# Blockwise FP4 quantiser: one Newton step fewer, and the square on VectorE instead of ScalarE

## The chip, the cores and the metric

One Trainium2 chip, 8 cores. Every core runs the same program on its own two sequences of the batch (4,096 tokens of 16 x 2,048). The metric is the device time of the slowest core in microseconds.

## What is computed

A transformer block on x (16 x 2048 x 1024, fp32): layer norm, then a linear-attention branch with an MLP (s) and an FP4-quantised gated FFN (g), joined as x + s * silu(g).

```python
def fp4_quant_dequant(x):            # blocks of 16 along the last axis
    scale = max(max(|xb|) / 6, 1e-12)
    xn = xb / scale
    idx = searchsorted([0.25, 0.75, 1.25, 1.75, 2.5, 3.5, 5.0], |xn|)
    return GRID[idx] * sign(xn) * scale     # GRID = 0, .5, 1, 1.5, 2, 3, 4, 6
def fp4_linear(x, w):
    return quant(x) @ quant(w).T

xn = layernorm(x)
# branch 1: rmsnorm, qkv, phi(t) = exp(-t*t/2), linear attention, projection,
#           then rmsnorm, conv1 (1024 -> 2048), gelu, conv2 (2048 -> 1024)
s = attn_block(xn)
# branch 2: inner size 2816
h = silu(fp4_linear(xn, w_gate)) * fp4_linear(xn, w_up)
g = silu(fp4_linear(h, w_down))
out = x + s * g
```

## The kernel before

The kernel writes its instructions into one list for each engine (`S.add("v", ...)` for VectorE, `"sc"` for ScalarE, `"pe"` for TensorE, `"sy"` for the DMA queue of SP). Each engine works through its list strictly in that order and waits on counting semaphores. So where an instruction stands in the list decides what it can hold up. A core has 32 tiles of 128 tokens. The stages run one after the other:

- P0: statistics of the layer norm. P1: qkv, attention and projection.
- P2, the convolution stage: 8 superblocks of 4 tiles. A superblock has a front (for each tile: load x2b, ScalarE casts it to x2f at L875, VectorE scales it at L878, 8 transposes and 8 copies), then 128 conv1 matmuls with 16 Gelus on ScalarE (L910, L919), then for each tile 32 conv2 matmuls (L938) and six VectorE instructions, the first of which is the bias add at L947. Between them the quantisation of the gate and up weights is pumped in: `pump(55)` behind each tile of the front and `pump(25)` behind each tile of the back takes that many steps of a generator. It works on 44 chunks of 128 rows x 1024 columns, each as one pair of quantisers of 512 columns. The chunks have a load and a store of their own on SP's queue.
- P25, the down-weight stage: 8 chunks of 128 x 2816, each as two pairs of 704 columns, with nothing else beside them.
- A1, the gate stage: for each tile VectorE normalises (L1031) and one pair of quantisers (512 columns) runs; then 8 transposes and 8 copies xqf on ScalarE (L1048, L1055), 48 gate matmuls (L1066) and 6 SiLUs on ScalarE (L1075).
- A2, the up stage: for each tile two loads (xqu at L1103, the gate at L1107), 48 up matmuls (L1120), 6 copies on ScalarE (L1129), the product gld * up on VectorE (L1132), two pairs of quantisers (704 columns) one behind the other; then, for the tile before, 22 transposes and 22 copies hqf (L1152, L1158) and the store of hqT_h (L1161). In the lists this "back" of tile t - 1 stands behind the "front" of tile t, and the loads of tile t + 1 stand behind the store of tile t - 1 on SP's queue.
- B: the down matmuls and the output.

The quantiser (`quant_gen`) is one chain. VectorE: maximum of each block (L648), scale (L651), a first guess for its reciprocal by integer arithmetic (L654 to L662), then Newton rounds of three small instructions each (L669, L672, L676), on one number a block (32 or 44 of them in a partition). Then u = x / scale (L682). ScalarE: u2 = u * u (L686, Square), Sign of u (L689), Sign of u2 against three thresholds (L692, L695, L698). VectorE compares u2 with four other thresholds (L701, L704, L707, L710: called "checks" below), adds the Signs (L713, L716), puts the two together (L719), multiplies the sign by the scale (L723) and writes the result (L728). `run_gens` and the chunk generator let two quantisers take turns, instruction by instruction.

A chunk of the pumped quantiser has 33 generator steps: number 1 to 5 for the maximum to the guess, 12 for the Newton rounds, 18 for u, 19 to 23 for the five ScalarE instructions, 24 to 27 for the checks, 28 to 32 for the rest and 33 for the store.

Of the kernel before, what the change touches and what calls it, by code (L numbers as in the profile page):

```python
# [11 lines left out]
AF = mybir.ActivationFunctionType  # L12
# [48 lines left out]
S = Sched()  # L61
# [60 lines left out]
def build():  # L122
    global S
    S = Sched()
# [21 lines left out]
    with ExitStack() as es:  # L146
# [28 lines left out]
        for nm, src, dst, csem in [("qkv", "L0_attn_qkv_w", "qkv_bf", "CQ"),  # L175
# [4 lines left out]
                  inc=csem, ev="cast_" + nm)  # L180
# [8 lines left out]
              waits=["iota_id"], inc="V", ev="identb")  # L189
# [4 lines left out]
        for oc in range(HID // P):  # L194
# [3 lines left out]
                inc="VR", ev=("ld_vrows" if oc == HID // P - 1 else None))  # L198
        S.add("v", lambda v: v.memset(ones1[:], 1.0), inc="V", ev="ones1")
        with ExitStack() as p0:  # L200
# [5 lines left out]
            for i, nm in enumerate(("s1", "s2", "gm", "pb", "c2b")):  # L206
                for h in range(2):
# [3 lines left out]
                        waits=["ones1", "ld_vrows"] + ([prev] if prev else []),  # L211
                        inc="PE", ev="repm%d_%d" % (i, h))
                    S.add("v", lambda v, nm=nm, h=h: v.tensor_copy(
                        reps[nm][:, 512 * h:512 * (h + 1)], rep_ps[:]),
                        waits=["repm%d_%d" % (i, h)], inc="V", ev="repc%d_%d" % (i, h))
                    prev = "repc%d_%d" % (i, h)
            for t in range(NT):
# [3 lines left out]
                    waits=[S.gev("p05v%d" % (t - 2), "V")], inc="XA%d" % b, ev="p05x%d" % t)  # L221
                S.add("sc", lambda sc, b=b: sc.activation(xsq[b][:], xa[b][:], AF.Square),
                      waits=["p05x%d" % t, S.gev("p05v%d" % (t - 2), "V")],
# [415 lines left out]
        def quant_gen(q, src_ap, dst_ap, W, waits_src, done_ev):  # L639
# [25 lines left out]
            yield  # L665
            yv = wi.bitcast(F32)
            prev = e("wi2")
            for it in range(4):
                S.add("v", lambda v, yv=yv, prev=prev: v.tensor_tensor(w2, sca, yv, op.mult),  # L669
                      waits=[prev], inc="V", ev=e("w2a%d" % it))  # L670
                yield
                S.add("v", lambda v, it=it: v.tensor_scalar(w2, w2, -1.0, 2.0, op.mult, op.add),  # L672
                      waits=[e("w2a%d" % it)], inc="V", ev=e("w2b%d" % it))
                yield
                dst = rec if it == 3 else w1
                S.add("v", lambda v, yv=yv, dst=dst, it=it: v.tensor_tensor(dst, yv, w2, op.mult),  # L676
                      waits=[e("w2b%d" % it)], inc="V", ev=e("nr%d" % it))
                yv = w1
                prev = e("nr%d" % it)
                yield  # L680
            rb = rec.rearrange("p nb -> p nb ()").broadcast_to([P, nb, 16])
            S.add("v", lambda v: v.tensor_tensor(  # L682
                u.rearrange("p (nb b) -> p nb b", b=16), x3, rb, op.mult),
                waits=[e("nr3")], inc="V", ev=e("u"))
            yield
            S.add("sc", lambda sc: sc.activation(u2, u, AF.Square),  # L686
                  waits=[e("u")], inc="SC", ev=e("u2"))
            yield
            S.add("sc", lambda sc: sc.activation(sgn, u, AF.Sign),  # L689
                  inc="SC", ev=e("sgn"))  # L690
            yield
            S.add("sc", lambda sc: sc.activation(s5, u2, AF.Sign, bias=thrB[:, 0:1]),  # L692
                  waits=[e("u2"), "thrB"], inc="SC", ev=e("s5"))
# [595 lines left out]
```

How the kernel before makes its waits and increments, by code:

```python
                def body(eng):  # L1261
                    for fn, waits, inc, amt in S.ops[key]:
                        for smn, val in waits:
                            eng.wait_ge(sems[smn], val)
                        ins = fn(eng)
                        if inc is not None and ins is not None:
                            ins.then_inc(sems[inc], amt)
```

## Time and profile before

| | us |
|---|---|
| median of the runs (2) | 7,250.89 |
| lowest, highest | 7,241.04, 7,260.75 |
| the profiled execution, its time | 7,273.16 |
| its span on the slowest core | 7,271.6 |
| spans of the eight cores | 7,212.9 to 7,271.6 |
| busy: VectorE | 3,821.7 (53%) |
| busy: TensorE matmul | 2,620.9 (36%) |
| busy: ScalarE | 2,226.5 (31%) |
| DMA, 16 engines, mean | 54 GB/s |

The profile shows one execution on its slowest core. Busy shares are means over stages that differ, so they say little by themselves; the windows by stage and the timeline say which wait ends last. A line such as L672 names the line of the kernel that issued an instruction. Timeline lines join neighbouring instructions of one kind ("x2"), and the bracket at their end tells how long the engine was idle before and what released it.

### The profile page before, as it was taken

To read this page: it belongs to the slowest core of one execution; us is meant where nothing else is said; L and a number is where in the kernel's file an instruction comes from. 1 tells how busy PE (TensorE), PEld (TensorE's weight loads), DVE (VectorE), ACT (ScalarE), POOL (GpSimd) and SP (SyncE) were. 2 spreads that over 40 slices of the span, in tenths; PEclk is the share of its full clock that TensorE was granted. 3 is DMA by queue.
4 is the path that set the end of the run, shared out by engine and by line. 5 is a ranking of instruction groups with operands and counts; after the bars stand their busy time and mean duration, and the time that the engine had idled before them with its cause. 6 is when DMAs were issued, how large, how long until landed. Compare 5 with 4: busy or idle time off the path is not lost.

```text
span 7271.6 us, 59859 instructions; the slowest of 8 cores (7212.9 to 7271.6 us)
## 1 busy us (share of the span) xinstructions
PE 2620.9 (36%) x10905; PEld 1125.2 (15%) x11098; DVE 3821.7 (53%) x9384; ACT 2226.5 (31%) x4379; POOL 3.2 (0%) x13
## 2 busy tenths in 40 slices
PE   0066456542303213373004445422222222222288
PEld 0022122211101101131001222111101110111033
DVE  0400320133576676525776666566676677667522
ACT  0133223321322322222224344323333333333211
POOL 0000000000000000000000000000000000000000
PEclk9988678866656656686556666655555555555599
DMA  8500010013011110010122222211101110111255
GB/s 98 139 24 24 33 46 21 18 44 77 28 39 34 37 38 31 33 32 26 48 56 80 79 85 82 88 50 41 41 27 41 41 41 27 41 41 41 70 168 174
DMA packets 227710, 396.17 MB, mean 54 GB/s; under 512 B 147861, under 2 KB 147989, under 8 KB 217626
## 3 DMA queue, kind: packets, MB, share of 16 engines
q1 hardware_dynamic: 226778, 375.57, 16.3%
q0 software_dynamic: 576, 16.78, 2.1%
q8 instruction: 111, 1.82, 0.1%
q14 instruction: 245, 2.01, 0.1%
HBM read 246.44 MB, written 145.33 MB: 54 GB/s over the span
## 4 chain that ended last, share of the span: by engine, by line
PE 29%; issue 25%; DVE 21%; ACT 11%; DMA 7%; SPq 5%; DVEq 1%; ACTq 0%
PE gps L1066 5%; PE ups L1120 5%; PE kvg_ps L394 4%; PE c1ps L910 3%; PE d_ps L1218 3%; SPq L195 2%; PE c2ps L938 2%; DMA xqu<-xqT_h 2%; PE q_ps L443 2%; PE prA L588 1%; ACT qb_s L695 1%; DVE gld L1132 1%; DMA hln<-hqT_h 1%; PE xp4t L1152 1%; DMA winw<-L_ffn_w_up 1%
## 5 line engine op out<-in xcount | busy, mean ns | idle before, releaser
L1152 PE MATMUL xp4t<-ident_b,hq 128*128 128x128 bf16 x704 | 178.8, 261 | 1368.1 <-ACT hqf L1158 1283.3
L1120 PE MATMUL ups<-wquT,xqu 128*128 128x512 bf16 (+1 forms) x1504 | 364.9, 410 | 243.3 <-DMA xqu<-xqT_h 208.3
L1132 DVE TENSOR_TENSOR gld<-gld,up 128x2816 f32<-128x2816 f32 x32 | 98.9, 3092 | 608.1 <-ACT up L1129 608.1
L363 DVE SCALAR_TENSOR_TENSOR xn<-xn,rstd_all,rep_s 128x1024 bf16<-128x1024 f32 x32 | 41.1, 1284 | 693.0 <-ACT xn L352 693.0
L890 PE MATMUL xp2t<-ident_b,xn 128*128 128x128 bf16 x256 | 65.1, 265 | 923.2 <-DVE xn L878 389.7
L1048 PE MATMUL xp3t<-ident_b,xq 128*128 128x128 bf16 x256 | 67.8, 265 | 893.9 <-DVE xq L728 864.8
L1066 PE MATMUL gps<-wqgT,xqf 128*128 128x512 bf16 (+1 forms) x1504 | 362.4, 408 | 31.7 <-ACT xqf L1055 31.7
L686 ACT ACTIVATE qb_u<-qb_u 128x704 f32<-128x704 f32 x128 | 101.1, 790 | 828.8 <-DVE qb_u L682 828.0
L1218 PE MATMUL d_ps<-wqdT,hln 128*128 128x512 bf16 x1379 | 322.2, 394 | 85.0 <-DMA hln<-hqT_h 80.7
L394 PE MATMUL kvg_ps<-qkvT,fmsup 128*128 128x512 bf16 x992 | 303.8, 471 | 29.7 <-ACT fmsup L378 25.0
L1152 PEld LDWEIGHTS xp4t<-ident_b,hq 128*128 128x128 bf16 x704 | 73.3, 104 | 1471.8 <-issue 1470.9
L910 PE MATMUL c1ps<-fm,conv1T 128*128 128x512 bf16 x1000 | 246.9, 410 | 102.7 <-ACT hddf L919 95.3
L938 PE MATMUL c2ps<-conv2T,hddf 128*128 128x512 bf16 x1004 | 228.6, 387 | 56.6 <-DVE s_t L964 18.1
L1129 ACT COPY up<-ups 128x512 f32<-128x512 f32 x192 | 105.4, 550 | 465.2 <-PE ups L1120 456.5
L686 ACT ACTIVATE qgw_u<-qgw_u 128x512 f32<-128x512 f32 x88 | 53.8, 629 | 604.4 <-DVE qgw_u L682 604.2
L1120 PEld LDWEIGHTS ups<-wquT,xqu 128*128 128x128 bf16 x1536 | 164.0, 108 | 441.3 <-issue 325.9
L1233 DVE TENSOR_TENSOR gfl<-gfl,sfl 128x1024 f32<-128x1024 f32 x32 | 39.2, 1226 | 335.1 <-ACT sfl L1230 335.1
L947 DVE TENSOR_TENSOR scc<-c2ps,rep_c2b 128x512 f32<-128x512 f32 x64 | 41.2, 686 | 326.0 <-PE c2ps L938 313.5
L1158 ACT COPY hqf<-xp4t 128x128 bf16<-128x128 bf16 x704 | 182.4, 265 | 86.5 <-PE xp4t L1152 53.8
L1066 PEld LDWEIGHTS gps<-wqgT,xqf 128*128 128x128 bf16 x1536 | 163.4, 108 | 227.9 <-issue 111.9
L1075 ACT ACTIVATE gate<-gps 128x512 f32<-128x512 f32 x192 | 107.8, 562 | 284.9 <-PE gps L1066 284.8
L596 DVE TENSOR_TENSOR x2w<-prA,rep_pb 128x512 f32<-128x512 f32 x32 | 22.1, 692 | 309.0 <-PE at L548 289.8
(243 smaller groups left out, 6874.9 us busy)
## 6 DMA issues: line engine op xcount, KB each, us to landing
xa<-x SPq DMA_DIRECT2D x160, 512.0 KB, 4.0
gate_h<-gate SPq DMA_DIRECT2D x32, 1408.0 KB, 5.7
gld<-gate_h SPq DMA_DIRECT2D x32, 1408.0 KB, 7.1
hqT_h<-hqf SPq DMA_DIRECT2D x32, 704.0 KB, 3.7
hln<-hqT_h SPq DMA_DIRECT2D x32, 704.0 KB, 5.7
out<-otl SPq DMA_DIRECT2D x32, 512.0 KB, 3.2
winw<-L_ffn_w_gate SPq DMA_DIRECT2D x22, 512.0 KB, 3.8
winw<-L_ffn_w_up SPq DMA_DIRECT2D x22, 512.0 KB, 3.9
```

What stands on the lines that cost most here:

```text
L195: S.add("sy", lambda sy, oc=oc: sy.dma_start(out=c1b_fm[:, oc:oc + 1], in_=g["L0_attn_conv1_b"][P * oc:P * (oc + 1)].rearrange("p -> p ()" ...
L394: S.add("pe", lambda pe, sup=sup, sp=sp, ic=ic, gg=gg: pe.matmul(kvg_ps[gg % 2][:], sup[:, 512 * ic + P * sp:512 * ic + P * (sp + 1)], qkv ...
L443: S.add("pe", lambda pe, sup=sup, qc=qc, ic=ic: pe.matmul(q_ps[0][:], qkvT[:, 3 * D * ic + P * qc:3 * D * ic + P * (qc + 1)], sup[:, 512 * ...
L686: S.add("sc", lambda sc: sc.activation(u2, u, AF.Square), waits=[e("u")], inc="SC", ev=e("u2"))
L910: S.add("pe", lambda pe, sup=sup, oc=oc, ic=ic: pe.matmul(c1_ps[oc % 2][:], conv1T[:, HID * ic + P * oc:HID * ic + P * (oc + 1)], sup[:, 5 ...
L938: S.add("pe", lambda pe, hdd=hdd, t=t, tt=tt, ic=ic, hh=hh: pe.matmul(c2_ps4[2 * (t % 2) + hh][:], hdd[:, 512 * ic + P * tt:512 * ic + P * ...
L1066: S.add("pe", lambda pe, b=b, ic=ic, cgo=cgo, cgw=cgw, cgi=cgi: pe.matmul(g_ps[cgi % 4][:, 0:cgw], xqf[b][:, P * ic:P * (ic + 1)], wqgT[:, ...
L1120: S.add("pe", lambda pe, b=b, ic=ic, cgo=cgo, cgw=cgw, cgi=cgi: pe.matmul(u_ps[cgi % 4][:, 0:cgw], xqu[b][:, P * ic:P * (ic + 1)], wquT[:, ...
L1132: S.add("v", lambda v, b=b: v.tensor_tensor(gld[b][:], gld[b][:], up_t[b][:], op.mult), waits=["a2_g%d" % t, "a2_ue%d_5" % t], inc="V", ev ...
L1152: S.add("pe", lambda pe, b=b, ic=ic: pe.transpose(xp4_ps[ic % 2], hq[b][:, P * ic:P * (ic + 1)], ident_b[:]), waits=tw, inc="PE", ev="a2_t ...
L1158: S.add("sc", lambda sc, b=b, ic=ic: sc.copy(hqf[b][:, P * ic:P * (ic + 1)], xp4_ps[ic % 2]), waits=fw, inc="SC", ev="a2_fme%d_%d" % (t, ic))
L1218: S.add("pe", lambda pe, b=b, t=t, ic=ic, hh=hh: pe.matmul(d_ps[2 * (t % 2) + hh][:], hln[b][:, P * ic:P * (ic + 1)], wqdT[:, D * ic + 512 ...
```

## The change

One Newton round of the quantiser is dropped (three instead of four). u * u is computed on VectorE by a product of u with itself instead of by Square on ScalarE. Sign of u on ScalarE, which stood behind Square and needed no wait of its own, now waits for u. Everything else, the numbers of steps taken by `pump` included, stays; a chunk of the pumped quantiser has 30 generator steps instead of 33.

```diff
             yv = wi.bitcast(F32)
             prev = e("wi2")
-            for it in range(4):
+            NRI = 3
+            for it in range(NRI):
                 S.add("v", lambda v, yv=yv, prev=prev: v.tensor_tensor(w2, sca, yv, op.mult),
...
-                dst = rec if it == 3 else w1
+                dst = rec if it == NRI - 1 else w1
...
             S.add("v", lambda v: v.tensor_tensor(
                 u.rearrange("p (nb b) -> p nb b", b=16), x3, rb, op.mult),
-                waits=[e("nr3")], inc="V", ev=e("u"))
-            yield
-            S.add("sc", lambda sc: sc.activation(u2, u, AF.Square),
-                  waits=[e("u")], inc="SC", ev=e("u2"))
+                waits=[e("nr%d" % (NRI - 1))], inc="V", ev=e("u"))
+            yield
+            S.add("v", lambda v: v.tensor_tensor(u2, u, u, op.mult),
+                  waits=[e("u")], inc="V", ev=e("u2"))
             yield
             S.add("sc", lambda sc: sc.activation(sgn, u, AF.Sign),
-                  inc="SC", ev=e("sgn"))
+                  waits=[e("u")], inc="SC", ev=e("sgn"))
```

## Rows read from the trace of the kernel before

**Rows 1.** Windows by stage: window, length; busy of PE, PEld, DVE, ACT, POOL; PEclk, DMA, GB/s

```profile
1786.00:3355.00 1569.00, 540.54 (x2260) 233.44 (x2304) 932.92 (x2600) 445.38 (x857) 0.00 (x0) 0.66 0.10 33
3355.00:3824.00 469.00, 0.00 (x0) 0.00 (x0) 351.56 (x865) 121.22 (x160) 0.00 (x0) 0.50 0.18 52
3824.00:4747.00 923.00, 430.26 (x1760) 190.04 (x1792) 587.84 (x1760) 359.96 (x769) 0.00 (x0) 0.68 0.25 84
4747.00:6865.00 2118.00, 538.81 (x2208) 237.31 (x2240) 1503.47 (x3488) 769.68 (x1536) 0.00 (x0) 0.58 0.10 37
```

**Rows 2.** Timeline, one tile of A1: start, length, engine, line [idle before]

```profile
4213.43 1.14 ACT L686 ACTIVATE qa_u<-qa_u 128x512 f32<-128x512 f32 x2
4214.15 0.95 DVE L701 TENSOR_SCALAR qa_tA<-qa_u 128x512 f32<-128x512 f32 x2 [8.38 <-ACT qa_u L686]
4214.47 1.14 ACT L689 ACTIVATE qa_sgn<-qa_u 128x512 f32<-128x512 f32 x2
...
4215.51 1.32 ACT L692 ACTIVATE qa_s<-qa_u,thrB 128x512 f32<-128x512 f32 x2
...
4217.95 1.32 ACT L698 ACTIVATE qa_u<-qa_u,thrB 128x512 f32<-128x512 f32 x2
4218.63 1.29 DVE L713 TENSOR_TENSOR qa_s<-qa_s 128x512 f32<-128x512 f32 x2
...
4223.44 1.29 DVE L728 SCALAR_TENSOR_TENSOR xq<-qa_tA,qa_tB 128x512 bf16<-128x512 f32 x2
```

**Rows 3.** Timeline, one tile of A2, and the page's group of L682 (the first line)

```profile
L682 DVE TENSOR_TENSOR qb_u<-gld,qb_rec 128x704 f32<-128x704 f32 x128 | 108.4, 888 | 0.3 <-DVE qb_rec L676 0.3
...
6031.53 0.39 DVE L676 TENSOR_TENSOR qb_w<-qb_wi,qb_w 128x44 f32<-128x44 f32 x2
...
6032.44 0.39 DVE L676 TENSOR_TENSOR qb_w<-qb_w 128x44 f32<-128x44 f32 x2
...
6034.57 1.70 DVE L682 TENSOR_TENSOR qb_u<-gld,qb_rec 128x704 f32<-128x704 f32 x2
6035.55 1.59 ACT L686 ACTIVATE qb_u<-qb_u 128x704 f32<-128x704 f32 x2 [14.77 <-DVE qb_u L682]
...
6037.25 0.53 DVE L701 TENSOR_SCALAR qb_tA<-qb_u 128x704 f32<-128x704 f32 x1 [0.28 <-ACT qb_u L686]
6037.69 1.69 DVE L704 SCALAR_TENSOR_TENSOR qb_tB<-qb_u,qb_tA 128x704 f32<-128x704 f32 x2
6038.41 1.64 ACT L692 ACTIVATE qb_s<-qb_u,thrB 128x704 f32<-128x704 f32 x2
...
6041.51 1.64 ACT L698 ACTIVATE qb_u<-qb_u,thrB 128x704 f32<-128x704 f32 x2
...
6067.73 3.09 DVE L1132 TENSOR_TENSOR gld<-gld,up 128x2816 f32<-128x2816 f32 x1 [17.12 <-ACT up L1129]
```

**Rows 4.** Timeline, VectorE, one chunk of the convolution stage

```profile
2037.98 1.29 DVE L682 TENSOR_TENSOR qgw_u<-winw,qgw_rec 128x512 f32<-128x512 f32 x2 [0.27 <-DVE qgw_rec L676]
...
2040.10 0.43 DVE L701 TENSOR_SCALAR qgw_tA<-qgw_u 128x512 f32<-128x512 f32 x1 [0.17 <-ACT qgw_u L686]
2040.44 0.69 DVE L704 SCALAR_TENSOR_TENSOR qgw_tB<-qgw_u,qgw_tA 128x512 f32<-128x512 f32 x1
```

**Rows 5.** Timeline, VectorE's first bias add in superblocks one, two, five, six

```profile
1982.46 1.29 DVE L947 TENSOR_TENSOR scc<-c2ps,rep_c2b 128x512 f32<-128x512 f32 x2 [41.62 <-PE c2ps L938]
...
2262.35 1.29 DVE L947 TENSOR_TENSOR scc<-c2ps,rep_c2b 128x512 f32<-128x512 f32 x2 [21.38 <-PE c2ps L938]
...
3071.48 1.29 DVE L947 TENSOR_TENSOR scc<-c2ps,rep_c2b 128x512 f32<-128x512 f32 x2 [35.35 <-PE c2ps L938]
...
3157.12 1.29 DVE L947 TENSOR_TENSOR scc<-c2ps,rep_c2b 128x512 f32<-128x512 f32 x2 [42.24 <-PE c2ps L938]
```

**Rows 6.** Timeline, TensorE, the up matmuls of two tiles of A2

```profile
6387.80 10.58 PE L1120 MATMUL ups<-wquT,xqu 128*128 128x512 bf16 x47 [5.52 <-DMA xqu<-xqT_h]
6452.78 12.20 PE L1120 MATMUL ups<-wquT,xqu 128*128 128x512 bf16 x47 [5.34 <-DMA xqu<-xqT_h]
```

## The prediction

> **What bounds the kernel now.** I read the windows by stage first. The reader is to see which engine is full where. Quantisation sits in four stretches, in all 5,079 us of 7,271.6 [rows 1]: the convolution stage with the weight quantiser woven in (1,569 us, VectorE busy 933), the down-weight stage (469 us, VectorE 352), the gate stage A1 (923 us, VectorE 588) and the up stage A2 (2,118 us, VectorE 1,503). No engine fills any of them, so the next view is the timeline of one tile, in which one looks for the idle gap that follows the longest unbroken chain.
>
> In A1 one tile takes 27 us. ScalarE does the last SiLU of the tile before (L1075), only then Square; VectorE has been ready for 8.38 us and waits for that Square [rows 2]. From the first Square (4213.43) to the end of VectorE's last quantiser instruction (4223.44 + 1.29 = 4224.73) 11.30 us pass; the transposes, the gate matmuls and the next SiLUs follow one after the other. So the tile's loop is closed through ScalarE's place in the quantiser, not through VectorE's sum of work.
>
> In A2 a tile takes about 66 us. VectorE works through two pairs of quantisers. ScalarE's last Sign of the second pair ends at 6041.51 + 1.65 = 6043.16 [rows 3]; behind it, in ScalarE's order, stand the 22 copies of hqf, behind these on SP's queue the store of hqT_h and the load of xqu, then the up matmuls and the up copies, and then the product (L1132) that starts the next tile. VectorE's own tail ends before all that: the product starts at 6067.73 after 17.12 us of idle time [rows 3]. What counts in A2 is how early ScalarE gets done with the second pair.
>
> In the down-weight stage nothing but the quantiser runs, and VectorE paces it.
>
> In the convolution stage VectorE works through quantiser steps, and once a superblock (512 tokens) it waits for the convolution matmuls at the bias add, for 21 to 42 us [rows 5].
>
> **The change, part by part.** It has three parts: one Newton step (three small VectorE instructions) less, the square moved from ScalarE to VectorE, and with it the first Sign released by u, no longer by its place behind Square. No DMA is added. Two quantisers always run in step, so I cost pairs, and by distance of starts, since VectorE's instructions overlap a little.
>
> *Newton step.* The same line of two successive rounds starts at 6031.53 and 6032.44: 0.91 us for a pair [rows 3]. I take 0.9 for the narrower ones too (32 instead of 44 elements; both are nearly all fixed cost).
>
> *Square on VectorE.* The trace has no product of a large tensor with itself. The nearest rows are the two-tensor instructions of the same shape and type: pairs of 512 columns start 4.81 / 4 = 1.20 us apart [rows 2], for 704 columns one takes 0.89 and two 1.70, so the second starts 0.81 after the first, a pair every 1.6 [rows 3]. Bounds: not below the one-input check, started 0.44 before its follower (6037.25, 6037.69), 0.88 a pair [rows 3]; not above two passes, 3.2. I take 1.60 and 1.20, as the operation is a plain product of two reads.
>
> *The wait that goes.* At 704 columns u starts at 6034.57 and the second check's pair (tB) at 6037.69, 3.12 later, with waits for Square inside [rows 3]. Afterwards: 1.60 + 1.60 + 0.88 = 4.08. So VectorE loses 0.96 there and wins 0.91: +0.05 a pair. At 512 columns before: 2040.44 - 2037.98 = 2.46; after: 1.20 + 1.20 + 2 x 0.34 (2040.10 to 2040.44) = 3.08; with the Newton step -0.3 a pair [rows 4].
>
> *A2.* First pair: +0.05. Second pair: u starts 0.91 earlier. From u's start to ScalarE's end 8.59 us pass now. Afterwards: both Signs of u from 0.98 on, where Square starts now; they are out of the way in time. The next Sign waits for the first square, started at 1.60, done 0.89 later, seen 0.1 later: 2.59. Then three pairs of Signs: 3.10 for two of them (6038.41 to 6041.51) and 1.65: ended at 7.34. That is 1.25 earlier. Sum: 0.05 - 0.91 - 1.25 = -2.1 us a tile. The 22 copies, the store and the load behind them all move up with it. VectorE's end does not, but it has 17 us of idle time to spare. 31 tiles: -65 us.
>
> *A1.* Afterwards, counted from the end of SiLU (4213.43, where Square starts now): two Signs of u 1.04, two of the first threshold 1.22, the next of the first quantiser done at 1.04 + 1.22 + 0.71 = 2.97 [rows 2]; the sum s5 + s6 starts at 3.07. The last Sign ends at 4.80 (now from 4214.47 to 4217.95 + 1.32 = 4219.27); its user starts at 4.9, six more starts of 0.60 and 0.69 to the end: 9.2. Now it is 11.30, so -2.1 us a tile; 31 tiles: -65 us. This costs the square and the four checks at nothing. What hides them is the 8.38 us wait: 1.2 + 4.48 (4214.15 to 4218.63) - 0.9 = 4.8 us fit in. Without that cover the 4.8 would come back. What is late next is the sum that waits for the Sign; ScalarE stays in the chain.
>
> *Down weights.* 16 pairs at +0.05: +1 us.
>
> *Convolution stage.* 44 chunks, one pair each: -0.3 x 44 = -13 us. The generator has 33 steps a chunk now and 30 afterwards, and the number of steps taken at each place (55 and 25) is fixed. So the quantiser is used up after 1,452 / 320 = 4.5 superblocks now and 1,320 / 320 = 4.1 afterwards, and each superblock's front ends at another step of a chunk. At the end of the front now: steps 22, 12, 2 and 25, with waits at the bias add of 41.6, 21.4, 24.5 and 38.1 us, and 35.3 in the fifth, where the quantiser has just run out; 42.2 without any quantiser [rows 5] (its four rows are the first, second, fifth and sixth superblock). The wait is short where VectorE still has the tail of a chunk to do after ScalarE's last Sign. Afterwards: steps 10, 0, 20, 10, and none left in the fifth. By the nearest now: 21.4, about 30, 41.6, 21.4, 42.2. Sum 157 against 161: -4 us. The fronts of the fifth superblock lose cover: three tiles that each wait some 4.6 us for x2f where two waited 3; but fewer fronts then end among ScalarE's steps. I put +2 on that, between -10 and +20.
>
> *The clock of TensorE.* The up matmuls of one tile (47 of 48) take between 10.58 and 12.20 us [rows 6], because they start after a pause: the granted clock over A2 is 0.58 of full [rows 1], a mix of its two levels, 1.2 and 2.4 GHz, and a tile's burst begins at the lower one. Starting a tile earlier moves this switch. It is worth up to 0.8 us a tile either way from the middle. I take 0.2 us lost in each of 62 tiles (the pause gets shorter, the slow stretch does not start later): +12 us.
>
> **Sum:** -65 - 65 + 1 - 13 - 4 + 2 + 12 = -132 us. On the profiled execution's 7,273.2 that is 7,141; its ratio to the median of the runs is 7,250.9 / 7,273.2 = 0.997. So **7,119 us**, 1.8% less. All durations come from that one execution. A change of about 2% (145 us) is what a measurement of this kernel can tell from none, and the forecast lies just inside.
>
> **Rivals.**
> 1. *VectorE sets the time after all.* For: it is the busiest engine, and it gets a large instruction more. Against: 8.4 us idle a tile in A1 and 17 in A2. Then only VectorE's differences count: A1 -0.3 x 32, A2 +0.05 x 64, down +1, convolution -13: -19 us, 7,232.
>    The Trainium skill's page "Perfetto Trace Analysis", section "Identifying the Most-Contended Engine", says to find the engine with the highest occupancy and to optimise that one first. By it, loading VectorE (53% busy) to relieve ScalarE (31%) gives nothing, which is this rival. The timeline rows speak against it, so it gets one chance in ten.
> 2. *The clock gives the gain back.* In all 62 tiles the slow stretch grows by the full 0.8 instead of 0.2: +37 us, 7,156. The other way round, -0.8 everywhere: -62 us, 7,057, which is faster by more than 2%; half of it reaches 7,088.
> 3. *The convolution stage falls apart.* The new phase of the steps gives one long wait more at the bias add (+20) and uncovers the fronts (+20): 7,160.
> 4. *Slower: the product of a tensor with itself is dear.* If both reads of one tile took a second pass, a pair would cost 3.2 and 2.4 us. Added: A2 64 x 1.6 = 102, down 16 x 1.6 = 26, convolution 44 x 1.2 = 53, A1 nothing (it still fits the cover): +181 - 132 = +49, 7,300. It decides from an extra of about 1.2 us a pair at 704 columns. For it speaks only that no row shows such a product.
>
> **Numbers.** Forecast as reckoned (7,095 to 7,145): 0.60. Rival 1: 0.10. Rival 2, worse 0.10, better 0.10. Rival 3: 0.07. Rival 4: 0.03. The range 7,085 to 7,180 holds the forecast, the worse side of 2, rival 3 and part of the better side of 2. Faster by over 2% means below 7,106: the lower third of the forecast and the better side of rival 2, together 0.28. Slower by over 2% (above 7,396) would need more than any case gives: 0.02. Within 2%: 0.70.
>
> **What the profile after would show.** A1's tile period 2 us shorter, VectorE waiting at the sum s5 + s6 (L713 of now) and not at the first check. A2's product (L1132) 2 us sooner after the last one, and the idle time before it about as much shorter. ScalarE busy for less by the time of Square. The five waits at the bias add near 21, 30, 42, 21 and 42. The prediction is wrong if A1 or A2 keeps its period, if the square takes far from 0.89 / 0.69 us, or if the matmul bursts of A1 and A2 change by more than 0.4 us on average.

## The result, and the profile after

The changed kernel takes 7,129.3 us (median of 11 runs, 7,099.8 to 7,186.2) against 7,271.2 for the kernel before beside it (10 runs, 7,241.0 to 7,313.0). The ratio is 0.9803, with a 95% interval of 0.9770 to 0.9837. The forecast, 7,119 over 7,250.9, was 0.9818. The profiled execution took 7,108.6 us; its eight spans have a mean of 7,095.4 against 7,236.9, which is 141.4 us less, where 132 were forecast. The gain is clear of noise; whether it is above or below 2% is not decided, since the interval holds 0.98.

Span by stage, each a mean over the eight cores of the profiled execution:

| stage | before | after | change | forecast |
|---|---|---|---|---|
| convolution (first x2f to the first down weight) | 1,571.0 | 1,543.6 | -27.4 | -15 |
| down weights | 457.1 | 455.0 | -2.1 | +1 |
| A1, from its first tile to its 32nd | 838.8 | 778.5 | -60.3 | -59 with the clock's +6 |
| A2, from its first product to its 32nd | 2,038.0 | 1,990.5 | -47.5 | -59 with the clock's +6 |
| all the rest | 2,332.0 | 2,327.9 | -4.1 | 0 |

On some executions a part of the cores runs some stages at a lower granted clock; below, a median is over all runs of a kernel, a ratio leaves such executions out, and a stage time of a single kernel is that of its cores where this is not so (so the convolution stage is 1,568 before and 1,539 after, and not the means of the table).

Windows by stage, slowest core of the kernel after (columns as in [rows 1]):

```profile
1782.00:3335.00 1553.00, 565.00 (x2304) 237.98 (x2303) 938.86 (x2423) 402.89 (x768) 0.00 (x0) 0.65 0.10 34
3335.00:3794.00 459.00, 0.00 (x0) 0.00 (x0) 361.57 (x804) 101.37 (x128) 0.00 (x0) 0.50 0.17 50
3794.00:4650.00 856.00, 445.19 (x1792) 190.76 (x1792) 596.38 (x1629) 326.68 (x705) 0.00 (x0) 0.70 0.26 89
4650.00:6713.00 2063.00, 563.52 (x2234) 239.95 (x2234) 1535.75 (x3232) 688.99 (x1401) 0.00 (x0) 0.58 0.10 38
```

Beside [rows 1], VectorE is busy *longer* in every stage (1,536 against 1,503 us in A2), and every stage is shorter. ScalarE is busy for less. The mean granted clock in A2 is 0.58 as before; the bursts of matmuls in it did change, as shown below.

One tile of A1, timeline (start, length, engine, line, idle time before it):

```profile
4207.79 0.38 ACT L1076 ACTIVATE gate<-gps 128x256 f32<-128x256 f32 x1 [0.28 <-PE gps L1067]
4208.07 1.14 ACT L690 ACTIVATE qa_sgn<-qa_u 128x512 f32<-128x512 f32 x2
4210.34 1.32 ACT L696 ACTIVATE qa_s<-qa_u,thrB 128x512 f32<-128x512 f32 x2
4211.15 1.30 DVE L714 TENSOR_TENSOR qa_s<-qa_s 128x512 f32<-128x512 f32 x2 [5.75 <-ACT qa_s L696]
4211.56 1.32 ACT L699 ACTIVATE qa_u<-qa_u,thrB 128x512 f32<-128x512 f32 x2
4216.07 1.28 DVE L729 SCALAR_TENSOR_TENSOR xq<-qa_tA,qa_tB 128x512 bf16<-128x512 f32 x2
```

The first Sign starts at 4208.07, right behind the tile's last SiLU. VectorE has done square and checks and waits 5.75 us for the sum (L714, before L713). From the first Sign to VectorE's last end (4216.07 + 1.28) 9.28 us pass. The forecast had 9.2 for it, and [rows 2] had 11.30.

One tile of A2, second pair, timeline:

```profile
5976.59 1.69 DVE L683 TENSOR_TENSOR qb_u<-gld,qb_rec 128x704 f32<-128x704 f32 x2
5977.57 1.59 ACT L690 ACTIVATE qb_sgn<-qb_u 128x704 f32<-128x704 f32 x2 [16.30 <-DVE qb_u L683]
5978.20 1.68 DVE L687 TENSOR_TENSOR qb_u<-qb_u 128x704 f32<-128x704 f32 x2
5979.23 1.68 ACT L693 ACTIVATE qb_s<-qb_u,thrB 128x704 f32<-128x704 f32 x2
5979.80 0.95 DVE L702 TENSOR_SCALAR qb_tA<-qb_u 128x704 f32<-128x704 f32 x2
5982.36 1.64 ACT L699 ACTIVATE qb_u<-qb_u,thrB 128x704 f32<-128x704 f32 x2
5997.32 12.02 PE L1121 MATMUL ups<-wquT,xqu 128*128 128x512 bf16 x48 [5.06 <-DMA xqu<-xqT_h]
```

The pair of squares takes 1.60 us from start to start (5978.20 to 5979.80), as reckoned. From u to the end of the last Sign 7.41 us pass (5982.36 + 1.64 - 5976.59), against 7.34 reckoned and 8.59 before. But then the up matmuls: 12.02 us.

The square itself, two of its four groups (duration in ns, lowest/median/highest):

```profile
L687 DVE TENSOR_TENSOR qb_u<-qb_u x128: 880/883/885, 4676.1 to 6692.1; 128x704 f32<-128x704 f32 x128
L687 DVE TENSOR_TENSOR qgw_u<-qgw_u x88: 680/683/686, 1788.2 to 2956.1; 128x512 f32<-128x512 f32 x88
```

A tensor times itself costs what a product of two tensors costs ([rows 3]: 888 ns at 704 columns). Rival 4 falls with these lines.

### The profile page after: what moved, and what is told of

It reads as the page before. It is cut to its first block, busy times and chain, and to the rows that moved or that the text cites. A ratio compares the mean times of both kernels' runs of the same rounds, so it can differ in the third digit from the quotient of the medians.

```text
span 7107.0 us, 58492 instructions; the slowest of 8 cores (7082.1 to 7107.0 us)
## 1 busy us (share of the span) xinstructions
PE 2689.6 (38%) x11098; PEld 1128.7 (16%) x11098; DVE 3879.1 (55%) x8760; ACT 2052.9 (29%) x4067; POOL 3.2 (0%) x13
## 4 chain that ended last, share of the span: by engine, by line
PE 31%; issue 25%; DVE 20%; ACT 12%; DMA 7%; SPq 5%; DVEq 1%; ACTq 0%
PE ups L1121 5%; PE gps L1067 5%; PE kvg_ps L394 4%; PE c1ps L911 3%; PE d_ps L1219 3%; SPq L195 2%; PE c2ps L939 2%; DMA xqu<-xqT_h 2%; PE q_ps L443 2%; PE prA L588 2%; DVE gld L1133 1%; DMA hln<-hqT_h 1%; PE xp4t L1153 1%; DMA winw<-L_ffn_w_up 1%; DMA winw<-L_ffn_w_gate 1%
## 5 line engine op out<-in xcount | busy, mean ns | idle before, releaser
L1121 PE MATMUL ups<-wquT,xqu 128*128 128x512 bf16 (+1 forms) x1536 | 391.1, 425 | 229.0 <-DMA xqu<-xqT_h 196.0
L1067 PE MATMUL gps<-wqgT,xqf 128*128 128x512 bf16 (+1 forms) x1536 | 377.4, 414 | 19.6 <-ACT xqf L1056 19.6
L690 ACT ACTIVATE qb_sgn<-qb_u 128x704 f32<-128x704 f32 x128 | 101.1, 790 | 838.9 <-DVE qb_u L683 838.2
L939 PE MATMUL c2ps<-conv2T,hddf 128*128 128x512 bf16 x1024 | 244.5, 404 | 61.2 <-DVE qgw_w L670 30.5
L690 ACT ACTIVATE qgw_sgn<-qgw_u 128x512 f32<-128x512 f32 x88 | 53.7, 630 | 610.0 <-DVE qgw_u L683 610.0
L948 DVE TENSOR_TENSOR scc<-c2ps,rep_c2b 128x512 f32<-128x512 f32 x64 | 41.2, 685 | 342.0 <-PE c2ps L939 335.2
```

Of the source, the lines that this page charges most:

```text
L690: S.add("sc", lambda sc: sc.activation(sgn, u, AF.Sign), waits=[e("u")], inc="SC", ev=e("sgn"))
L939: S.add("pe", lambda pe, hdd=hdd, t=t, tt=tt, ic=ic, hh=hh: pe.matmul(c2_ps4[2 * (t % 2) + hh][:], hdd[:, 512 * ic + P * tt:512 * ic + P * ...
L1067: S.add("pe", lambda pe, b=b, ic=ic, cgo=cgo, cgw=cgw, cgi=cgi: pe.matmul(g_ps[cgi % 4][:, 0:cgw], xqf[b][:, P * ic:P * (ic + 1)], wqgT[:, ...
L1121: S.add("pe", lambda pe, b=b, ic=ic, cgo=cgo, cgw=cgw, cgi=cgi: pe.matmul(u_ps[cgi % 4][:, 0:cgw], xqu[b][:, P * ic:P * (ic + 1)], wquT[:, ...
```

## The experiments

All ten kernels, each beside the kernel before on the same chip:

| kernel | median, us (runs) | ratio to before, 95% interval |
|---|---|---|
| e1_newton_only | 7,138.1 (4) | 0.9848 [0.9752, 0.9944] |
| e2_square_only | 7,238.3 (10) | 0.9940 [0.9887, 0.9992] |
| e3_old_phase | 7,141.2 (4) | 0.9833 [0.9738, 0.9929] |
| e4_busy_a2 | 7,115.0 (5) | 0.9656 [0.9539, 0.9773] |
| e5_early_xqu | 6,968.3 (5) | 0.9522 [0.9451, 0.9594] |
| e6_busy_a1 | 7,126.1 (4) | 0.9789 [0.9723, 0.9856] |
| e7_early_weights | 7,015.8 (4) | 0.9618 [0.9547, 0.9688] |
| e8_all | 6,742.6 (7) | 0.9250 [0.9197, 0.9304] |
| e9_two_outputs | 6,973.2 (4) | none (7,305.5 before); judged by its stages |
| e10_all_two | 6,690.5 (4) | 0.9148 [0.9069, 0.9228] |

These intervals are too wide for effects of 10 to 50 us. The stage times are the fine instrument: in the kernel after, A1 and A2 agree within some 4 us from core to core, the convolution stage within some 8.

### The two halves of the change: e1_newton_only and e2_square_only

The first keeps the three Newton rounds and gives the square back to ScalarE, the second keeps the square on VectorE and four rounds.

```diff
 # e1_newton_only, against the kernel after
-            S.add("v", lambda v: v.tensor_tensor(u2, u, u, op.mult),
-                  waits=[e("u")], inc="V", ev=e("u2"))
+            S.add("sc", lambda sc: sc.activation(u2, u, AF.Square),
+                  waits=[e("u")], inc="SC", ev=e("u2"))
...
-                  waits=[e("u")], inc="SC", ev=e("sgn"))
+                  inc="SC", ev=e("sgn"))
 # e2_square_only, against the kernel after
-            NRI = 3
+            NRI = 4
```

> Edit: the kernel before with three Newton rounds instead of four; the square stays on ScalarE (Square). Theory A, the chain that closes each tile runs through ScalarE's place in the quantiser: A1 does not move (31 tiles in 839 us, clock of TensorE aside), because VectorE only gets ready earlier for a Square that waits for SiLU. A2 loses 0.91 us in each of two pairs, 1.8 us a tile, 56 us over 31 tiles; the down-weight stage loses 16 x 0.91 = 15 us; the convolution stage 44 x 0.88 = 39 us and a few us by the phase of its steps. Sum about -110 us, ratio to the kernel before 0.985. Rival B, VectorE's sum of work sets the time: A1 loses 31 x 0.9 = 27 us too, sum -137 us, ratio 0.981.

> Edit: the changed kernel with four Newton rounds as before; the square is on VectorE. Theory A: A1 loses 2.1 us a tile, 65 us, as in the changed kernel, and does not feel the fourth round, which lies in VectorE's waiting time. A2: first pair +0.96, the second pair's end on ScalarE 1.25 earlier: -0.3 us a tile, -9 us over 31 tiles. Down weights 16 x 0.96 = +15 us, convolution 44 x 0.63 = +28 us. Sum -31 us, ratio 0.996. Rival B: A1 +20, A2 +61, down +15, convolution +28: +124 us, ratio 1.017.

Stage times, us:

| | before | Newton only | square only | both (after) |
|---|---|---|---|---|
| convolution | 1,568 | 1,543 | 1,580 | 1,539 |
| down weights | 457 | 439 | 469 | 455 |
| A1 | 839 | 837 | 779 | 778.5 |
| A2 | 2,038 | 1,990 | 2,031 | 1,990.5 |

A1 is the clear verdict. Newton alone leaves it where it was; the square alone gives the whole 60 us, and the fourth Newton round costs nothing on top. What VectorE waits for in A1 (us in all, times, longest), on core 6, before:

```profile
DVE qa_tA L701 <- ACT qa_u L686: 263.2, 34, 9.0
```

and with Newton only:

```profile
DVE qa_tA L702 <- ACT qa_u L687: 293.0, 34, 9.9
```

Then on core 3, with the square only:

```profile
DVE qa_s L714 <- ACT qa_s L696: 167.2, 31, 6.5
```

and after, with both:

```profile
DVE qa_s L714 <- ACT qa_s L696: 195.9, 31, 7.4
```

With the Newton round gone VectorE only waits longer for ScalarE's Square, by 29.8 us. With the square moved it waits for the Signs, and the fourth round (31 x 0.9 = 28 us) comes out of that wait: 195.9 less 167.2 is 28.7. So A1's loop closes through ScalarE, and rival 1 is refuted there. The Trainium skill's page "Perfetto Trace Analysis", section "Identifying the Most-Contended Engine", would have the engine with the highest occupancy relieved first. This trace does not agree: VectorE, the busiest at 53%, got 64 squares more in A1 (it is at 55% of the span now), and A1 became 60 us shorter.

The down weights are the reverse case, the one stage that VectorE paces: -18 for the Newton round (1.1 us in each of 16 pairs) with the square on ScalarE and -14 (0.9) with it on VectorE, and +12 to +16 for the square. The -2.1 of both is the small rest of two opposite terms.

In A2, Newton alone already gives 48 us, the square alone 7, and both together no more than Newton alone. The chain says otherwise: it gets 1.9 us a tile shorter in the first (0.95 in each pair), 2.1 with both. The next experiments bear on that.

In the convolution stage both halves missed their numbers: -25 for the Newton round where 39 us less were expected, +12 for the square where 28 more were. The second is explained by its waits: on core 4 those for the bias add, the first of superblocks 1 to 5, come to 151.6 us (156.9 before, core 3) and those for x2f, without the first, to 69.4 (82.3 before). That is 18 us less, in a kernel whose only change is the square, with the old number of generator steps.

### The old phase of the pumped quantiser: e3_old_phase

Three empty generator steps put a chunk back to 33 steps, so that the pump stops where it stopped before.

```diff
+            for _ in range(3):
+                yield
```

> Edit: the changed kernel with three empty generator steps in place of the dropped round, so that a chunk has 33 steps again and each pump of the convolution stage ends at the place in a chunk where it ended before. The instructions are the same; only their order against the convolution's changes. Theory A: the mean time from the first x2f to A1 fell by 29.5 us in the changed kernel, of which the shorter pair explains 44 x 0.25 = 11 to 13 us and the phase the rest; with the old phase the stage is 16 us longer than in the changed kernel, the waits at the bias add are again near 41, 21, 24, 38, 35 us; ratio to the kernel before 0.9825. Rival: the phase brings nothing, ratio 0.980 as the changed kernel.

The convolution stage takes 1,532 us (1,529 to 1,533 on the eight cores), *less* than after's 1,539 (1,540 in e4, which has the same instructions there). A miss: 16 us more were expected. The new phase costs 7 us, where I had let it save 2 (-4 at the bias adds, +2 at x2f). What VectorE waits for in this stage, core 3, first the kernel after:

```profile
DVE xn L879 <- ACT x2f L876: 134.5, 19, 49.7
DVE qgw_am L648 <- DMA winw<-L_ffn_w_up: 86.9, 19, 6.0
DVE qgw_am L648 <- DMA winw<-L_ffn_w_gate: 86.4, 19, 6.5
DVE scc L948 <- DMA s_h<-s_t: 6.2, 2, 3.1
```

and then with the old phase:

```profile
DVE xn L881 <- ACT x2f L878: 117.4, 20, 47.8
DVE qgw_am L648 <- DMA winw<-L_ffn_w_up: 98.9, 22, 5.0
DVE qgw_am L648 <- DMA winw<-L_ffn_w_gate: 89.0, 20, 4.9
DVE scc L950 <- DMA s_h<-s_t: 2.3, 1, 2.3
```

| core 3, us | before | old phase, new quantiser | after |
|---|---|---|---|
| first bias add of superblocks 1 to 5 | 40.8 + 21.7 + 22.0 + 38.1 + 34.3 = 156.9 | 38.7 + 18.4 + 21.5 + 36.5 + 34.8 = 149.9 | 21.6 + 33.1 + 38.3 + 19.0 + 41.2 = 153.2 |
| x2f, without the first | 82.3 | 69.6 | 84.8 |
| load of a weight chunk (L648) | 190.7 (42 waits) | 187.9 (42) | 173.3 (38) |
| s_h at the bias add | 0 | 2.3 | 6.2 |

The old phase isolates a term that my sum did not have. With the places unchanged, the waits for the bias add are 7 us shorter and those for x2f 13. The kernel with the square alone shows the same two (5 and 13), so they come from the square and not from the Newton round: ScalarE now has 88 Squares less to do in this stage, and the Gelus and casts queued behind the quantiser come earlier. The new phase then gives back 3 and 15, and takes 15 from the load waits, because four more chunk starts come behind some other wait that covers their load (38 of 44 wait for it, not 42; the six that do not wait each stand a few instructions behind a wait for the bias add, x2f or s_h). The sum of the differences from after to the old phase (-3.3 - 15.2 + 14.6 - 3.9) is -7.8; the stages differ by 7 on the mean over the cores, by 11.7 on this one, so up to 4 us of it lie in smaller pieces.

### The clock in A2: e4_busy_a2

Twelve matmuls that nobody reads, into an unused PSUM tile, fill the pause in which TensorE waits for xqu.

```diff
+                for wi in range(NWARM if t >= 2 else 0):      # NWARM = 12
+                    S.add("pe", lambda pe: pe.matmul(
+                        w_ps[:], wquT[:, 0:P], wquT[:, 0:512],
+                        start=True, stop=True), waits=["a2_tp%d_21" % (t - 2)] if wi == 0 else [])
```

> Edit: the changed kernel with 12 matmuls into an unused PSUM tile in front of each tile's up matmuls in A2, where TensorE waits 5.1 us for the load of xqu. Theory A, clock: the 48 up matmuls took 11.75 us on average before and 12.35 in the changed kernel (core 3), because more of them ran at 1.2 GHz, and this took 0.6 of the 2.1 us a tile back. With the pause filled they run at 2.4 GHz nearly from their start: 10.6 to 11 us, so A2 is 1.5 us a tile, 45 us, shorter than in the changed kernel; ratio to the kernel before 0.974. Rival: the longer bursts come from something else (loads of weights, PSUM): they stay at 12.3 us, ratio 0.980, or above it by the time of the added matmuls if they outlast the pause.

A2 takes 1,917 us, 73.5 less than after, with 360 matmuls more (12 in each of 30 tiles); 45 less and bursts of 10.6 to 11 us were expected. Timeline, TensorE:

```profile
5535.55 4.00 PE L1115 MATMUL wps<-wquT 128*128 128x512 bf16 x12
5540.52 9.67 PE L1127 MATMUL ups<-wquT,xqu 128*128 128x512 bf16 x48 [0.96 <-DMA xqu<-xqT_h]
```

Windows of one tile; the value behind the five engines is the granted clock (0.50 is 1.2 GHz, 1.00 is 2.4 GHz). First the kernel after (transposes, the pause, then two stretches of the up matmuls):

```profile
5984.00:5993.00 9.00, 5.31 (x20) 2.09 (x20) 9.00 (x12) 5.52 (x23) 0.00 (x0) 0.50 0.01 3
5993.00:5997.00 4.00, 0.00 (x0) 0.00 (x0) 0.58 (x1) 0.00 (x0) 0.00 (x0) 0.50 0.90 302
5997.30:6001.30 4.00, 3.98 (x10) 1.45 (x11) 0.00 (x0) 0.26 (x1) 0.00 (x0) 0.50 0.65 270
6001.30:6005.30 4.00, 4.00 (x19) 1.68 (x17) 0.00 (x0) 1.10 (x3) 0.00 (x0) 0.90 0.00 0
```

and then this kernel (the twelve matmuls, the first up matmuls):

```profile
5535.60:5539.50 3.90, 3.90 (x12) 1.31 (x12) 1.50 (x2) 0.16 (x1) 0.00 (x0) 0.68 0.72 229
5540.50:5544.50 4.00, 3.98 (x19) 1.87 (x20) 0.00 (x0) 0.87 (x2) 0.00 (x0) 1.00 0.63 270
```

After: the burst begins at 1.2 GHz, ten matmuls in four microseconds. Here the fill-in matmuls take the slow stretch on themselves while the DMA is under way, and the burst runs at 2.4 GHz throughout, 9.67 us. The mean burst of 48 on core 3 was 11.8 before, 12.1 with Newton only, 12.35 after, 9.71 here. So the slow start costs 2.1 us a tile before and 2.7 after. The forecast's row of 10.58 was no fast burst, it only had less of the slow stretch. The Trainium skill's page "TensorE: Matmul & The Clock Gate", section "HAM oscillation — how this bites in real kernels", tells of waits for DMA between groups of matmuls after which the clock has to rise anew, and advises to order the loop so that TensorE does not lose it. The trace agrees, with 73.5 us for 30 pauses filled.

This also closes A2's sum. Means of 29 tiles of the timeline, us, on cores 1, 3, 4, 5 and 7 (Newton only: 1, 3 and 7; square only: 1, 4, 5 and 7):

| | before | Newton only | square only | after |
|---|---|---|---|---|
| product to the first pair's u | 9.86 | 8.90 | 9.83 | 8.89 |
| that u to the second pair's u | 22.52 | 21.57 | 23.48 | 22.54 |
| that u to the end of the last Sign | 8.57 | 8.57 | 7.43 | 7.43 |
| copies, and the way to the first up matmul | 13.08 | 13.10 | 13.07 | 13.10 |
| burst of 48 up matmuls | 11.76 | 12.10 | 11.66 | 12.26 |
| its end to the next product | 0.57 | 0.57 | 0.57 | 0.57 |
| period | 66.36 | 64.81 | 66.05 | 64.78 |

Before to after the chain gets 2.1 us shorter and the burst 0.5 longer (0.6 on core 3): -1.6 a tile, as -47.5 / 31 = -1.5 of the stage. Newton only has -1.9 and +0.3, the same -1.6. That both periods are equal is seen; why the slow stretch grows by just what the chain saves is not settled by these runs. It is no rule either: with the square only the chain is 0.2 shorter, and the burst does not grow.

### The pause itself: e5_early_xqu

On SP's queue the load of xqu for tile t + 1 is put ahead of the store of hqT_h of tile t - 1, which waits for the last copy of hqf. The load then waits only for the up matmuls that free its slot.

```diff
...
+                if t + 2 < NT:
+                    xq_load(t + 2)
                 S.add("sy", lambda sy, t=t, b=b: sy.dma_start(
                     out=g["hqT_h"][P * t:P * (t + 1), :], in_=hqf[b][:]),
```

> Edit: the changed kernel with the load of xqu for tile t + 2 placed on SP's queue ahead of the store of hqT_h of tile t, so that it no longer waits for that tile's 22 copies. Theory A, the chain of A2 runs from ScalarE's last Sign over the copies, then over SP's queue and this load, to the up matmuls: the pause of 5.1 us before the up matmuls falls to 0.3, and with VectorE idle for 16.3 us a tile all of it is gained: 31 x 4.8 = 149 us, A2 from 1,990 to about 1,840 us, idle time before the product from 16.3 to 11.5. Ratio to the kernel before 0.960. Rival, VectorE paces A2: A2 stays at 1,990 us, ratio 0.980.

A2 takes 1,815.6 us, 175 less than after. Timeline, TensorE:

```profile
5562.04 0.27 PE L1157 MATMUL xp4t<-ident_b,hq 128*128 128x128 bf16 x1 [0.16 <-ACT hqf L1163]
5562.28 11.26 PE L1125 MATMUL ups<-wquT,xqu 128*128 128x512 bf16 x48
```

The burst follows the last transpose and waits for nothing. In after, that wait was this (TensorE's waits in A2, core 3), and no such line is left here:

```profile
PE ups L1121 <- DMA xqu<-xqT_h: 153.6, 30, 5.7
```

Of the 178 us on core 3 (1,993.2 to 1,815.2) 153.6 are the pause; the other 25 are the clock: the mean burst is 11.55 instead of 12.35, 0.8 x 31 = 25. I had left that out of the 149 expected.

### The clock in A1: e6_busy_a1

36 unread matmuls behind the gate matmuls of each tile, before its transposes.

```diff
+                for wi in range(NBUSY if t >= 1 else 0):      # NBUSY = 36
+                    S.add("pe", lambda pe: pe.matmul(
+                        w3_ps[:], wqgT[:, 0:P], wqgT[:, 0:512], start=True, stop=True))
```

> Edit: the changed kernel with 36 matmuls into an unused PSUM tile between a tile's gate matmuls and the next tile's transposes in A1, where TensorE pauses for 10 us. Theory A, clock: A1's 48 gate matmuls take 11.8 us because they begin at 1.2 GHz; in A2 the filled pause brought 12.3 down to 9.7 us. Here the 8 transposes lie between the added matmuls and the gate matmuls and keep TensorE busy only in part, so I expect most but perhaps not all of it: 9.7 to 10.5 us, A1 31 x 1.3 to 2.1 = 40 to 65 us shorter than in the changed kernel (778), ratio 0.972 to 0.975. Rival, the transposes let the clock fall again: bursts stay at 11.8 us, ratio 0.980.

A1 takes 772, 6 less than after; 40 to 65 were expected. A miss. Timeline from the filler to the burst:

```profile
4204.04 7.93 PE L1046 MATMUL w3ps<-wqgT 128*128 128x512 bf16 x36
4214.12 0.60 PE L1054 MATMUL xp3t<-ident_b,xq 128*128 128x128 bf16 x2 [2.14 <-DVE xq L730]
4217.69 11.44 PE L1072 MATMUL gps<-wqgT,xqf 128*128 128x512 bf16 x48 [0.61 <-ACT xqf L1061]
```

and windows, the transposes and the start of the burst:

```profile
4212.00:4217.60 5.60, 2.07 (x8) 0.82 (x8) 5.41 (x19) 2.12 (x8) 0.00 (x0) 0.72 0.00 0
4217.70:4221.70 4.00, 4.00 (x11) 1.45 (x12) 4.00 (x19) 0.28 (x1) 0.00 (x0) 0.55 0.17 66
```

The filler runs at 2.4 GHz. Then come 5.6 us with 2.07 us of transposes in them, and in these the granted clock falls (0.72 is their mean), so that the burst starts at 1.2 GHz again. The fill ended 5.7 us before the burst, where that of e4 ended 1.0 us before it; this is what the rival on record had said. The mean burst fell only from 11.73 to 11.63.

### The loads of the convolution stage: e7_early_weights and e9_two_outputs

The load of the next weight chunk is issued before the present chunk is quantised, not after it; e9 has a second output buffer wqw in addition, so that a chunk need not wait for the store of the last.

```diff
 # e7_early_weights
...
+                if i == 0:
+                    wq_load(*args)
+                if i + 1 < len(chunks):
+                    wq_load(*chunks[i + 1])
 # e9_two_outputs, in addition
-            wqw = [wqw0, wqw0]
+            wqw = [wqw0, e2(nc.sbuf_tensor("wqw1", [P, D], BF16))]
...
-                                  (["wq_st%d" % (ui - 1)] if ui >= 1 else []) +
+                                  (["wq_st%d" % (ui - 2)] if ui >= 2 else []) +
```

> Edit: the changed kernel with each weight chunk's load issued one chunk ahead (both buffers exist already). Theory A, VectorE's order paces the convolution stage and the down-weight stage: each of the 38 waits of 4.5 us for winw and of the 7 of 8 us for win is on the path: -171 us in the convolution stage (1,540 to about 1,370), -56 us in the down-weight stage (455 to about 400), ratio 0.949. Rival, the convolution's matmuls and Gelus pace the stage: what is saved at the loads comes back as longer waits at the bias add, then less than half of the 171 us is seen, ratio above 0.960.

> The early-weights kernel once more, and in addition a second buffer for the quantised chunk (wqw), so that a chunk waits for the store of the chunk before the last and no longer for that of the last. Read in the early-weights run: in the convolution stage VectorE still waits 45.8 + 41.4 = 87.2 us, 38 times 2.3 us, at the block maximum (L648), and the line names the store of wqw as what ends it; before the loads were moved it was 173.3 us there, each wait as long as the store and the load behind it. Theory (the shortfall of that run against its forecast was this second wait, which the load had covered up): the 87 us go, with 10 to 25 us of them given back at the bias add, at x2f and at s_h: convolution stage 62 to 77 us shorter than its 1471 on undisturbed cores, so 1394 to 1409. The other stages stay (A1 778, A2 1990, down weights 397). Rival (what follows sets the pace anyway, the wait only moves to the convolution matmuls): less than 30 us shorter, above 1441.

The down-weight stage became 57 us shorter (397.5), as forecast. The convolution stage takes 1,471, 68 less than after, not 171. By its numbers (less than half of the 171 us, a ratio above 0.960) the rival came true and not theory A. VectorE's waits there, core 3:

```profile
DVE xn L885 <- ACT x2f L882: 138.7, 23, 45.5
DVE qgw_am L648 <- DMA wqg_h<-wqw: 45.8, 20, 2.6
DVE qgw_am L648 <- DMA wqu_h<-wqw: 41.4, 18, 2.6
DVE scc L954 <- DMA s_h<-s_t: 14.0, 7, 3.0
```

By its mechanism the rival did not: the waits for the convolution matmuls at the bias add stay (316.6 us after, 315.1 here, core 3), and only 16 us come back, 8 at x2f and 8 at s_h. The 173.3 us at the block maximum did not go elsewhere in the main. Half of them, 87.2, are still at the same instruction and have another name, the store of wqw: store and load ran side by side, and the profile names only the later one. In the kernel after, core 3, one store is issued at 2045.25 and lands at 2047.47, the load behind it is issued at 2045.75 and lands at 2049.62, and VectorE goes on at 2049.85. With the second buffer:

```profile
DVE xn L885 <- ACT x2f L882: 153.5, 26, 47.0
DVE scc L954 <- DMA s_h<-s_t: 25.8, 9, 5.0
```

The wait at L648 is gone; 15 us are back at x2f, 12 at s_h and 6 at the bias add. That is 54 net, and the stage goes from 1,471 to 1,411 (the other 6 us are in no wait that I followed), just below the 62 to 77 us that were expected.

### Everything together: e8_all and e10_all_two

e8 is e5, e6 and e7 in one, with unread matmuls of 256 columns between the transposes of A1 and A2 as well, so that the clock does not fall there. e10 has the second wqw too.

```diff
...
+                    if t >= 1:
+                        S.add("pe", lambda pe: pe.matmul(
+                            w3_ps[:, 0:256], wqgT[:, 0:P], wqgT[:, 0:256], start=True, stop=True))
```

> Edit: the changed kernel with the early xqu load, the early weight loads, the filled pause in A1, and in A1 and A2 an added matmul of 256 columns into an unused PSUM tile behind each transpose (so that the slow clock ends before the up and gate matmuls begin, now that no pause for a load is left to fill in A2). Theory A, the terms are independent, since each shortens another stretch of a serial chain: -149 (xqu), -84 (A2's bursts from 12.3 to 9.7 us), -65 (A1's bursts), -227 (weights): -525 us, ratio 0.908. Rival: VectorE's idle time in A2 (16.3 us a tile) is nearly used up by 4.8 + 2.7, and the added matmuls delay the transposes, which ScalarE's copies wait for: A2 not below 1,880 us, ratio above 0.925.

> All the edits of the last combined kernel and the second buffer for the quantised chunk. Theory: the gain of the buffer adds to the others unchanged, since the convolution stage was the same there with and without them (1472 beside 1471): convolution stage 1394 to 1409, ratio to the kernel before about 0.925 - 70 / 7278 = 0.915. Rival: as for the kernel with the buffer alone, convolution above 1441 and ratio 0.921 or more. A1 stays at 745, A2 at 1757.

e8 falls short of its forecast: its spans are 413 us shorter than after's, not 525, and the ratio is 0.925, not 0.908. A2 gives all that it should (233 us, and its rival, not below 1,880, is refuted); the weights give 129 of 227, for the reason just shown, A1 gives 33 of 65, and 18 us lie in stages that nothing was done to.

In A2 the sum closes: the mean burst is 9.67 us, 2.68 x 31 = 83 under after, and 153.6 of pause, which would be 1,754; measured 1,757. A1 has bursts of 10.72 on average, 1.01 x 31 = 31 less, and takes 745, 33 less than after. Timeline, one burst of A2 and one of A1:

```profile
5542.51 9.67 PE L1140 MATMUL ups<-wquT,xqu 128*128 128x512 bf16 x48
...
3979.15 10.37 PE L1081 MATMUL gps<-wqgT,xqf 128*128 128x512 bf16 x48 [0.39 <-ACT xqf L1070]
```

What the matmuls between the transposes do, windows of A2 (transposes, then their end) and of A1 (the end of the transposes):

```profile
5535.00:5540.40 5.40, 5.37 (x29) 1.88 (x29) 5.40 (x8) 3.56 (x14) 0.00 (x0) 0.50 0.01 3
5540.40:5542.50 2.10, 1.93 (x13) 0.74 (x13) 2.10 (x3) 1.50 (x7) 0.00 (x0) 0.98 0.02 4
...
3977.00:3979.00 2.00, 1.72 (x10) 0.55 (x8) 1.98 (x13) 1.33 (x5) 0.00 (x0) 0.55 0.04 4
```

In A2 the clock has risen before the burst begins. In A1 it still falls among the transposes, for a part of them only, and 1 us a tile is left on average (10.72 beside 9.67).

The convolution stage is 1,472 in e8 and 1,410 in e10, so the parts add. e10, at 0.9148 of the kernel before (forecast 0.915), is the fastest kernel of this study.

## Why the prediction was right, point by point

- **A1, -65 and +6 for the clock.** Right in mechanism and size. 31 x (9.28 - 11.30) = -63; the burst did not change (11.74 and 11.73) where 0.2 had been put. Measured -60.3.
- **A2, -65 and +6.** The chain is right: from u to u +0.02 for +0.05, the first u 0.97 earlier for 0.91, ScalarE's end 1.14 earlier for 1.25, in all the -2.1 reckoned. The clock term was mis-sized: the burst grew by 0.5 us (11.76 to 12.26) instead of 0.2, +16 instead of +6. Measured -47.5 against -59. In all, the clock cost 16 us where I had 12, but all in one stage, and there by more than the 0.4 us that I had named as a sign against the forecast.
- **Bounds of the clock.** "Worth up to 0.8 us a tile either way" came from two bursts of [rows 6], both of which began at 1.2 GHz (granted clock 0.50 in the first 2 us of the shorter and in the first 4 us of the longer). A burst wholly at 2.4 GHz takes 9.67, so the better side reached to about -2.1 us a tile. The range held because the start of the burst did not move that way.
- **Down weights, +1.** Measured -2.1. The Newton pair is worth 0.9 to 1.1 us here, for 0.91, and the square 0.8 to 1.0, for 0.96.
- **Convolution, pairs -13, bias adds -4, x2f +2.** Measured -27.4. The step "by the nearest now" was right in its numbers and not in its reason. The five waits came as forecast (21.6, 33.1, 38.3, 19.0, 41.2 for 21.4, 30, 41.6, 21.4, 42.2), and x2f rose by 2.5. But each is a sum of two things that I did not see: relief of ScalarE (-7, -13), which the kernel with the square alone shows by itself, and the new phase (+3, +15). The terms that were missing altogether are the 17 us less at the chunk loads and the 6 more at s_h. On core 3: -13 - 3.7 + 2.5 - 17.4 + 6.2 = -25.4, and its stage went from 1,566.4 to 1,541.0, which is -25.4 too. The -13 in it is the forecast's term; it was not measured by itself, and is what the waits leave over.
- **The total.** -141 for -132: the gain was 12 larger in the convolution stage, 3 in the down weights, 1 in A1 and 4 in stages that should not have moved, and 12 smaller in A2. So it came out near by errors of both signs, which is luck: a gain in the convolution stage from terms that I did not have made up for the clock in A2.
- **The rivals.** 1 falls (A1 followed ScalarE, by the two halves). Of 2, the clock gave back 16 us, nearer to the 12 of the forecast than to the 50 of its worse side. 3 did not come: the new phase costs 7, not 40. 4 falls by the durations of the square.

## What to carry to other kernels

Moving work onto the busiest engine can pay where the loop closes through another: find the instruction whose wait closes the tile, count what the move puts in front of it and behind it, and check that the receiving engine has idle time at that place, not on average. A wait's name is only the last of its causes; before you price its removal, look for the second one that ran beside it, as the store beside the load here. And where matmuls come in bursts, price the burst at both clocks, from a burst that is known to be wholly at the higher one.

## What the runs showed of the hardware

- The slow start of the matmul bursts is dear here: 2.7 us (core 3, after) on a burst that takes 9.67 at 2.4 GHz, 83 us in A2. A pause of 5 us on TensorE filled with twelve useless matmuls made A2 73.5 us shorter.
- In e6 eight transposes did not hold the clock: 2.07 us busy in 5.6 us, and the mean granted clock there was 0.72, then 0.55 in the first 4 us of the burst. With matmuls of 256 columns between them it was back at 0.98 by the burst in A2; in A1 it still fell for a part of them.
- Two kernels whose chains in A2 differ by 0.2 us a tile (Newton only, and after) had the same stage time of 1,990 us: the longer bursts took the difference. With the square alone a chain shorter by 0.2 us kept its gain. So a small saving in the chain can vanish in the clock, and it need not.
